# The 32x32 block inverse of a gated delta-rule layer: sums along contiguous memory at sizes 8 and 16, with transposed blocks kept in used places of X

## The reference

```python
mixed = silu(causal_conv4(hidden_states @ w_qkv))      # 256 -> 8192 channels
q, k, v = split(mixed); q = l2norm(q) * DK ** -0.5; k = l2norm(k)
beta = sigmoid(b); g = -exp(A_log) * softplus(a + dt_bias)
def step(Sm, inp):                                     # 128 steps of the recurrence
    q_, k_, v_, g_, b_ = inp
    Sm = Sm * exp(g_)[..., None, None]
    kv = einsum('bhk,bhkv->bhv', k_, Sm)
    delta = (v_ - kv) * b_[..., None]
    Sm = Sm + einsum('bhk,bhv->bhkv', k_, delta)
    o = einsum('bhk,bhkv->bhv', q_, Sm)
    return Sm, o
```

## Time and profile before

| what | value |
|---|---|
| runs of the kernel | 2265.43 us median of 3 (2264.45 to 2272.63) |
| the profiled execution | 2256.21 us, of which the span of the profile is 2254.1 us |
| PE busy | 2081.4 us (92%) |
| DVE busy | 1808.0 us (80%), 3552 instructions |
| ACT busy | 1507.3 us (67%) |
| POOL busy | 860.9 us (38%) |
| mean granted TensorE clock | 0.971 |

### The profile page before, as it was taken

The page is one execution under the profiler, slowest core; times in us unless marked ns, Lnnn a source line. Parts: engine busy times, 40 slices in busy tenths (PEclk is TensorE's granted clock), DMA queues, the critical chain, the costliest instruction groups (busy, mean ns, idle before and its releaser), DMA issues.

```text
span 2254.1 us, 49002 instructions
## 1 busy us (share of the span) xinstructions
PE 2081.4 (92%) x18124; PEld 1697.1 (75%) x18124; DVE 1808.0 (80%) x3552; ACT 1507.3 (67%) x3585; POOL 860.9 (38%) x762
## 2 busy tenths in 40 slices
PE   4559999999999999999999999999888899999998
PEld 3337888888888888888888888887775466666676
DVE  6889898988989898898989889897335777767765
ACT  4546777777677777767777776775667666565632
POOL 1533435435444543534444353441343123213232
PEclk8769999999999999999999999999999999999999
DMA  3422233232222323223232332302243012322232
GB/s 77 94 72 48 69 58 80 53 75 65 49 73 54 81 54 73 66 49 80 47 81 57 70 68 49 87 15 57 75 134 133 1 66 76 104 94 72 90 138 85
DMA packets 274636, 161.54 MB, mean 72 GB/s; under 512 B 209353, under 2 KB 246753, under 8 KB 269281
## 3 DMA queue, kind: packets, MB, share of 16 engines
q1 hardware_dynamic: 274400, 158.41, 26.9%
HBM read 122.43 MB, written 35.91 MB: 70 GB/s over the span
## 4 chain that ended last, share of the span: by engine, by line
issue 31%; PE 29%; POOL 18%; DVE 14%; ACT 5%; DMA 2%; SPq 1%; POOLq 0%; DVEq 0%; ACTq 0%
PE ps L1748 4%; POOL EB L496 4%; PE ps L1358 4%; POOL SM L581 3%; DVE A L912 3%; PE ps L1360 3%; PE ps L1359 3%; PE ps L1491 2%; POOL EB L500 2%; POOL SZ L583 2%; POOL Q L559 2%; POOL WL L474 2%; PE ps L1525 2%; POOL SM L588 2%; PE ps L1660 1%
## 5 line engine op out<-in xcount | busy, mean ns | idle before, releaser
L912 DVE SCALAR_TENSOR_TENSOR A<-ps,CW,A 128x508 f32<-128x508 f32 (+2 forms) x768 | 515.9, 734 | 102.8 <-ACT A L674 97.7
L576 POOL TENSOR_SCALAR SM<-SM 128x8 f32<-128x8 f32 x64 | 12.6, 196 | 855.3 <-ACT DL L693 855.3
L1491 PE MATMUL ps<-WO,DL 128*128 128x256 f32 x1008 | 241.2, 391 | 16.9 <-ACT TTF L814 9.8
L1358 PE MATMUL ps<-XH,WH 128*128 128x512 f32 x512 | 220.0, 430 | 28.0 <-DVE A L912 27.5
L1491 PEld LDWEIGHTS ps<-WO,DL 128*128 128x128 f32 x1008 | 187.4, 192 | 50.0 <-ACT DL L680 21.1
L1360 PE MATMUL ps<-XH,WL 128*128 128x512 f32 x512 | 205.8, 402 | 0.0
L1359 PE MATMUL ps<-XL,WH 128*128 128x512 f32 x512 | 205.3, 401 | 0.0
L693 ACT ACTIVATE DL<-SZ 128x128 f32<-128x128 f32 x512 | 152.2, 298 | 77.2 <-issue 48.0
L859 ACT ACTIVATE SC<-ps,A 128x128 f32<-128x128 f32 x512 | 142.1, 387 | 51.3 <-DVE A L1263 50.7
L1130 DVE TENSOR_TENSOR SZ<-SZ,ps 128x512 f32<-128x512 f32 x128 | 84.9, 683 | 107.7 <-PE ps L1525 107.7
L1115 DVE TENSOR_TENSOR BP<-ps,EB 128x512 f32<-128x512 f32 x256 | 158.3, 681 | 3.3 <-ACT EB L668 3.3
(11 more groups left out here) (229 smaller groups left out, 5674.1 us busy)
## 6 DMA issues: line engine op xcount, KB each, us to landing
EB<-decay_rows SPq DMA_DIRECT2D x128, 256.0 KB, 4.7
WE<-expert_halves SPq DMA_DIRECT2D x32, 1024.0 KB, 5.4
x_blocks<-BP SPq DMA_DIRECT2D x256, 32.0 KB, 1.6
X<-x_blocks SPq DMA_DIRECT2D x16, 512.0 KB, 6.4
tt_blocks<-TI SPq DMA_DIRECT2D x16, 512.0 KB, 2.6
tn_blocks<-TM SPq DMA_DIRECT2D x16, 512.0 KB, 2.6
TTF<-tt_blocks SPq DMA_DIRECT2D x256, 32.0 KB, 1.9
expert_halves<-BP SPq DMA_DIRECT2D x8, 1024.0 KB, 6.3
```

The costliest lines, as they stand in the source:

```text
L912: dve.scalar_tensor_tensor(acc, ps(i, 0, [[128, 4], [1, 128 - s]]), at(CW, tile * 4 + 3 - s, [[1, 1]]), acc, ALU.mult, ALU.add).then_inc(s ...
L1358: pe.matmul(out, sa, ma, start=(kt == 0), stop=False)
L1491: t = pe.matmul(ps(7 - i, b * 256, [[1, 256]]), at(on_buf(k), (4 * i + 2 * b + v) * 128, [[1, 128]]), at(WO, (k // 4 % 2) * 512 + v * 256, ...
```

## The change

Sizes 2 and 4 stay. At sizes 8 and 16 the multiply now writes its terms with the summed index innermost, both factors are read along that index, and the sum reads TM without steps. For that one factor of each product must lie transposed:

- ACT gets `mirror(j)`, two copies within X: the upper right blocks of size 8 (128 numbers in each partition) and of size 16 (256 numbers) go transposed into the lower left of X, which the inverse doesn't read. It waits for the load of X and counts in a new semaphore `x_mir`. It stands in steps 4, 8, ..., 64, behind the two z copies (L686) and ahead of `v_tap3` and of `kq_tap3(n + 1)`.
- DVE gets two copies, between the first product and the second of each of the two sizes: the lower right inverse in TI goes transposed into the upper left of X, whose numbers are used by then (128 numbers at size 8, 256 at size 16). Their costs in the planner are 228 and 356.
- DVE waits for `x_mir` ahead of size 8 and ahead of size 16.
- `INV_OPS` rises from 41 to 43.

The number of terms of each product is as before. The diff, with the parts that only change a bound left out:

```diff
-INV_OPS = 41
+INV_OPS = 43
...
+                def mirror(j):
+                    act.wait_ge(sem["ld_xb"], 16 * (j + 1))
+                    act.activation(at(X, 8 * 32, [[528, 2], [32, 8], [1, 8]]), at(X, 8, [[528, 2], [1, 8], [32, 8]]),
+                                   ACT.Copy).then_inc(sem["x_mir"], 1)
+                    act.activation(at(X, 16 * 32, [[32, 16], [1, 16]]), at(X, 16, [[1, 16], [32, 16]]),
+                                   ACT.Copy).then_inc(sem["x_mir"], 1)
...
                     if s3 and not s1:
                         u2_copy(m, 0)
+                    if n % 4 == 0 and 4 <= n <= NSTEP:
+                        mirror(n // 4 - 1)
                     if sv:
                         v_tap3(vn, 0)
                     if n < EARLY:
...
-                    for s in (2, 4, 8):
+                    for s in (2, 4):
...
+                    dve.wait_ge(sem["x_mir"], 2 * j + 1)
+                    for it in range(2):
+                        dve.wait_ge(inv, done)
+                        dve.tensor_tensor(at(TM, it * 512, [[64, 8], [8, 8], [1, 8]]), at(TI, it * 528, [[32, 8], [0, 8], [1, 8]]),
+                                          at(X, it * 528 + 256, [[0, 8], [32, 8], [1, 8]]), ALU.mult).then_inc(inv, 1)
+                        done += 1
+                        yield 612
+                    dve.wait_ge(inv, done)
+                    dve.tensor_reduce(at(UT, 0, [[1, 128]]), at(TM, 0, [[8, 128], [1, 8]]), AX.X, ALU.add).then_inc(inv, 1)
+                    done += 1
+                    yield 1124
+                    dve.tensor_copy(at(X, 0, [[528, 2], [32, 8], [1, 8]]),
+                                    at(TI, 8 * 33, [[528, 2], [1, 8], [32, 8]])).then_inc(inv, 1)
+                    done += 1
+                    yield 228
+                    for it in range(2):
+                        dve.wait_ge(inv, done)
+                        dve.tensor_tensor(at(TM, it * 512, [[64, 8], [8, 8], [1, 8]]), at(UT, it * 64, [[8, 8], [0, 8], [1, 8]]),
+                                          at(X, it * 528, [[0, 8], [32, 8], [1, 8]]), ALU.mult).then_inc(inv, 1)
+                        done += 1
+                        yield 612
+                    dve.wait_ge(inv, done)
+                    dve.tensor_reduce(at(TI, 8, [[528, 2], [32, 8], [1, 8]]), at(TM, 0, [[8, 128], [1, 8]]), AX.X, ALU.add,
+                                      negate=True).then_inc(inv, 1)
+                    done += 1
+                    yield 1124
+                    dve.wait_ge(sem["x_mir"], 2 * j + 2)
                     for q4 in range(4):
                         k0, kn = 4 * q4, 16 - 4 * q4
                         dve.wait_ge(inv, done)
-                        dve.tensor_tensor(at(TM, 0, [[16 * kn, 4], [16, kn], [1, 16]]), at(X, k0 * 32 + 16, [[0, 4], [32, kn], [1, 16]]),
-                                          at(TI, k0 * 32 + k0, [[32, 4], [1, kn], [0, 16]]), ALU.mult).then_inc(inv, 1)
+                        dve.tensor_tensor(at(TM, 0, [[16 * kn, 4], [kn, 16], [1, kn]]), at(TI, k0 * 33, [[32, 4], [0, 16], [1, kn]]),
+                                          at(X, 16 * 32 + k0, [[0, 4], [32, 16], [1, kn]]), ALU.mult).then_inc(inv, 1)
...
-                        dve.tensor_reduce(at(UT, k0, [[1, 4], [16, 16]]), at(TM, 0, [[16 * kn, 4], [1, 16], [16, kn]]), AX.X,
-                                          ALU.add).then_inc(inv, 1)
+                        dve.tensor_reduce(at(UT, k0 * 16, [[1, 64]]), at(TM, 0, [[kn, 64], [1, kn]]), AX.X, ALU.add).then_inc(inv, 1)
...
+                    dve.tensor_copy(at(X, 0, [[32, 16], [1, 16]]), at(TI, 16 * 33, [[1, 16], [32, 16]])).then_inc(inv, 1)
+                    done += 1
+                    yield 356
                     for q4 in range(4):
                         i0, kn = 4 * q4, 4 * q4 + 4
                         dve.wait_ge(inv, done)
-                        dve.tensor_tensor(at(TM, 0, [[16 * kn, 4], [16, kn], [1, 16]]),
-                                          at(TI, 16 * 32 + 16 + i0, [[1, 4], [32, kn], [0, 16]]),
-                                          at(UT, 0, [[0, 4], [16, kn], [1, 16]]), ALU.mult).then_inc(inv, 1)
+                        dve.tensor_tensor(at(TM, 0, [[4 * kn, 16], [kn, 4], [1, kn]]), at(UT, 0, [[16, 16], [0, 4], [1, kn]]),
+                                          at(X, i0 * 32, [[0, 16], [32, 4], [1, kn]]), ALU.mult).then_inc(inv, 1)
...
-                        dve.tensor_reduce(at(TI, 16 + i0, [[1, 4], [32, 16]]), at(TM, 0, [[16 * kn, 4], [1, 16], [16, kn]]), AX.X,
+                        dve.tensor_reduce(at(TI, 16 + i0, [[32, 16], [1, 4]]), at(TM, 0, [[kn, 64], [1, kn]]), AX.X,
                                           ALU.add, negate=True).then_inc(inv, 1)
```

14 lines of the change are left out of this document (7 added, 7 removed).

## The result

The changed kernel takes 2270.41 us (median of 20 runs, 2263.91 to 2277.83) beside 2263.29 us for the kernel before (20 runs, 2256.57 to 2272.63). The ratio is 1.0038, with a 95% interval of 1.0027 to 1.0049: 7.1 us slower, inside the half per cent that the prediction called no change, and outside its range of 2230 to 2258 us. The forecast was 22 us faster. Step lengths to 0.01 us are taken between DVE's marks, the windows are rounded to 0.1 us.

What follows compares the result with a forecast made beforehand. DVE was taken to bound one step in four (n = 1 mod 4), steps 4 to 7 and step 9, PE the floor. Terms -24.1 - 3.3 + 2.1 + 3.9 - 2.7 + 0.1 = -24.0 us gave 2241.4 us, range 2230 to 2258.

Steps and rivals of the forecast that it cites:

- The multiplies: DVE's multiplies at sizes 8 and 16: two of 512 take 1.42 us as before, nothing added.
- The part on added waits: Step 4: ACT stands from 88.05 until X lands at 96.33 us; the first inverse begins 8.2 us late.
- Rival (b): Multiplies held behind POOL, as L1000 starts 0.5 us sooner, take the gain back: 2261.5 us, chance 0.17.
- The sums: DVE's sums without steps take 1.23, 0.96, 0.69 and 0.41 us by size, saving 5.23 us an inverse.
- Rival (a): Sums out of SBUF stay slow whatever the step, only added work remains: 2292 us, chance 0.07.
- The step without the race: Steps with n = 1 mod 4, thirteen groups: each falls by 1.85 us to PE's floor, -24.1 us.
- Step 43: Last step of the group, ACT busiest, DVE with 4.8 us to spare: DVE's savings worth nothing there.
- rival (c): More steps gain: step 43 0.5 us, also first inverse and step 9; 2231 us, chance 0.14.
- The first wait: Steps 4 to 8: 8.2 us wait for X less 4.3 us saved, +3.9 us, bounds +1 and +6.
- Step 9: DVE's throughout, with the same pieces: -3.3 us, leaving 25.6; bounds -2.5 and -5.2.
- ACT's copies: Two added copies take 0.95 us; PE loses 0.15 us in each of fourteen steps, +2.1 us.
- The end: Step 65, where DVE runs most of inverse 15 and PE waits for the gate: -2.7 us.

Runs made afterwards that it cites:

- the early wait: The changed kernel with both waits for x_mir moved to the head of the inverse, none ahead of size 8 or 16: 2225.98 us.
- the fastest kernel: The changed kernel with x_mir waits early, first ACT copies moved to step 5, POOL waiting ahead of L583 for DVE's second size 8 multiply: 2213.60 us.
- POOL's wait: POOL waits ahead of L583 for DVE's second size 8 multiply; added alone to the kernel before: 2249.28 us, ratio 0.9934.
- the first experiment: The kernel before with one added DVE wait, already holding, for ld_xb ahead of the first size 8 multiply: 2303.82 us, ratio 1.0195.
- the kernel before with POOL's wait one step too late: The kernel before with POOL waiting for DVE's second size 8 multiply, written one step too late, so the margin didn't shift: 2263.17 us.

## Why the prediction was wrong, point by point

- **The multiplies, "the same, nothing added": the step that failed.** In step 41 of after the four multiplies and the copy of size 8 take 3.14 + 0.83 + 3.79 = 7.76 us; with the early wait they take 1.42 + 0.72 + 1.42 = 3.56. These 4.2 us use up the 1.9 us that DVE would have had to spare and more: PE waits 2.6 us in that step, where before it waited 1.3. Over 13 groups the steps took 354.1 us in the profiled execution, before 336.3: +17.7 us instead of -24.1.
- **The wait ahead of size 8 had no price in the sum.** The part on added waits looked for a wait that has to be waited for, and found the one in step 4. A wait that holds takes 0.07 us, and the margin that it had to leave intact was 0.04 us. L950's start and L583's both stood in the trace of before, but the prediction read POOL only from L588 on the earlier trace rows, where it saw a multiply held already.
- **Rival (b) had the mechanism**, and 2261.5 us for it at a chance of 0.17. It had the wrong place and size. It expected one or two multiplies to be held because L1000 would come *sooner*; they came later. Held multiplies cost 40.7 us in the whole (after against the early wait), (b) had allowed about 20 us.
- **The sums** were right: 1.22, 0.95, 0.69 and 0.41 us by size. Rival (a) is out.
- **The step without the race** was right: 23.83 us, -2.04 us where -1.85 was forecast, from the kernel with the early wait. DVE idles 1.9 us there, forecast about 1.
- **Step 43**: given as nothing; it and the like of it fell by 0.3 us in each of 13 (318.7 to 314.3 us in after); rival (c) had 0.5.
- **The first wait**: +3.9 us forecast for steps 4 to 8 (bounds +1 and +6), +1.9 us measured (98.65 to 100.53 us). The first inverse was worth more than its own 4.3 us: with the stall away steps 4 to 8 fall to 92.7 us in the fastest kernel, in part since the first inverse of before had held multiplies too (L977's 768 and 512 terms took 1.79 and 1.80 us, L989's 1024 terms 2.07, where 0.95, 0.69 and 1.22 are usual): 5.6 us in sum over its twelve, 2.5 us in the fastest kernel. (The prediction called 89.10 to 150.30 us steps 4 to 7; step 7 begins at 143.7 and ends at 164.9. No term was built on that bound.)
- **Step 9**: -3.3 us forecast, -1.4 measured, and -5.5 us with POOL's wait: held multiplies again (its margin is +0.13 us in before and +0.47 in after; the kernel before gains 3.8 us there by POOL's wait alone).
- **ACT's copies**: 0.43 and 0.64 us, forecast 0.95 for both. Steps with n = 0 mod 4 grew by 0.04 to 0.07 us as a rule (step 40 from 23.73 to 23.77), forecast 0.15; step 8 grew by 0.7 us (22.83 to 23.53).
- **Gaps that no term had.** Steps 20, 36 and 52 of after are 0.7 to 1.7 us longer than their like, with gaps in which PE waits for nothing that the trace shows. ACT's copies aren't the cause, since kernels without them have the same gaps in the same steps: step 36 of the first experiment takes 28.22 us, and step 20 of the kernel before with POOL's wait one step too late 29.18 (PE, then the window):

```profile
463.26 0.32 PE L1568 MATMUL ps<-TTF,U 32*32 32x32 f32 x4 [2.44 <-issue]
```
```profile
460.40:489.60 29.20, 26.75 (x243) 22.50 (x237) 18.28 (x50) 15.43 (x40) 8.97 (x9) 0.88 0.18 38
```

The other steps of that kernel are nearly those of before, yet its profiled execution took 9.7 us more than that of before, 8.1 of them in the steps with n = 0 mod 4 (316.2 us, before 308.1); the medians lie 3.0 us apart. So these gaps come and go between executions, and the one profiled of before has none: 19 us between the two profiled executions and 7 between the medians don't contradict each other, but which part of the 12 us is theirs isn't shown. What they are stays open.
- **The end**: -2.7 us forecast for step 65. From its first joining matmul (L1544, L1581 in after) to the next step's it fell from 26.6 to 23.4 us, as forecast and a little more, although PE's wait for the gate at its end hardly changed (3.12 us before, 3.08 in after). But the next stretch took it back. Before, then after:

```profile
1556.00:1582.60 26.60, 23.34 (x215) 20.07 (x216) 24.55 (x30) 13.14 (x39) 4.56 (x4) 0.82 0.20 49
1582.60:1603.70 21.10, 20.70 (x214) 18.05 (x214) 8.46 (x11) 14.27 (x43) 5.21 (x5) 0.92 0.13 34
```
```profile
1575.20:1598.60 23.40, 19.15 (x213) 16.74 (x214) 21.75 (x32) 12.90 (x39) 4.00 (x4) 0.98 0.23 56
1598.60:1622.20 23.60, 23.19 (x214) 19.91 (x214) 7.83 (x11) 14.29 (x43) 5.21 (x5) 0.80 0.12 33
```

  The second stretch is PE's work, with a mean granted clock of 0.80 where before had 0.92, and takes 2.5 us more. From the mark of step 64 to the end of the span nothing is left of the gain: 719.8 us before, 719.7 in after.

Put together: the change is worth 33.6 us where the order at size 8's first pair is as before (the early wait), 37.1 us where it is lost on both sides (after against the kernel before with a wait: 44.2 - 7.1), and 35.7 us where it is made certain on both (46.5 - 10.8; this one has the first copies moved, which is worth 5.6 to 7.7 of it). The forecast of 24.0 us was too small for the change and blind to the race, which took back 40.7.

## What to carry to other kernels

Where DVE and POOL work on SBUF at the same time, compare the start of each DVE multiply or copy with the start of POOL's instruction beside it before adding anything ahead of either, and ask who was first: a margin of some hundredths of a microsecond is a condition of the time measured, and even a wait that already holds can turn it. Put such waits where nothing runs close behind them, or make the engine that has time to spare wait for the other's instruction. Of a new consumer ahead of an old instruction ask when its input landed in the *first* turn of the loop, not only in the steady ones.
